# Gathering slot rows for a mixture of experts: GpSimd no longer waits for each batch of gathers, SyncE waits for the batches and counts them

## What is computed

```python
g, idx = jax.lax.top_k(logits, 2)
gates = jax.nn.softmax(g, axis=-1)
# gates_full[n, e]: the gate of token n for expert e, 0 where e was not chosen
def body(acc, p):
    W1 = wf1 + mg1 * ws1 + hf1
    h = jnp.square(jnp.maximum(flat_x @ W1 + bb1, 0.0))
    W2 = wf2 + mg2 * ws2 + hf2
    return acc + ge[:, None] * (h @ W2 + bb2), None
```

## Time and profile before

| | |
|---|---|
| device time, median of 3 (lowest, highest) | 1060.32 us (1057.99, 1063.25) |
| device time of the profiled execution | 1058.72 us |
| its span in the profile | 1057.0 us |
| TensorE busy | 789.1 us, 75% of the span |
| VectorE busy | 734.7 us, 70% |
| ScalarE busy | 650.3 us, 62% |
| GpSimd busy | 648.9 us, 61% |
| mean granted TensorE clock | 0.894 of full speed |
| first gather of slot rows starts | 791.66 us |
| last scatter starts | 1036.77 us |

### The profile page before, as it was taken

One profiled execution on the slowest core, in us unless ns is written; L12 is line 12 of the kernel. 1 busy time (PEld: TensorE's weight loads), 2 busy tenths in 40 slices (PEclk: granted clock), 3 DMA queues, 4 the chain that ended last, 5 costly groups with the idle time before them and its releaser, 6 DMA issues. The chain is left out here.

```text
span 1057.0 us, 14281 instructions
## 1 busy us (share of the span) xinstructions
PE 789.1 (75%) x4918; PEld 640.0 (61%) x4919; DVE 734.7 (70%) x836; ACT 650.3 (62%) x1149; POOL 648.9 (61%) x359
## 2 busy tenths in 40 slices
PE   0559772887878878788887888557266988999991
PEld 0225331787767777787777777457154665777771
DVE  4898376999999999999999999763182111222224
ACT  0134886999999999899998999034141221222221
POOL 7436464799988999799998999222036454111110
PEclk9969665899999999899999999887558998999996
DMA  4012101121214112122121211699996721000005
GB/s 84 0 60 119 65 25 40 41 80 61 81 60 140 61 62 79 67 74 71 70 78 63 79 63 60 215 261 238 209 206 126 160 59 42 19 19 19 19 19 187
DMA packets 31902, 91.92 MB, mean 87 GB/s; under 512 B 7560, under 2 KB 15264, under 8 KB 30824
## 3 DMA queue, kind: packets, MB, share of 16 engines
q1 hardware_dynamic: 20792, 57.53, 16.4%
q0 software_dynamic: 8352, 27.07, 11.9%
q10 hardware_dynamic: 2704, 6.61, 1.9%
HBM read 77.67 MB, written 13.53 MB: 86 GB/s over the span
## 5 line engine op out<-in xcount | busy, mean ns | idle before, releaser
L1361 PE MATMUL ps<-ident,arena 128*128 128x128 f32 (+1 forms) x3390 | 435.3, 283 | 171.2 <-DVE arena L816 54.3
L1361 PEld LDWEIGHTS ps<-ident,arena 128*128 128x128 f32 (+1 forms) x3390 | 383.4, 144 | 230.7 <-issue 73.8
L557 POOL TENSOR_TENSOR arena<-arena 128x1024 f32<-128x1024 f32 x192 | 426.5, 2250 | 44.4 <-DVE arena L816 42.1
L816 DVE TENSOR_TENSOR_SCAN arena<-arena,ps 128x1024 f32<-128x1024 f32 x192 | 427.8, 2269 | 5.3 <-PE ps L1361 3.4
L1202 ACT ACTIVATE arena<-arena,neg_a 128x510 f32<-128x510 f32 x384 | 241.2, 710 | 0.0
L1031 DVE TENSOR_SCALAR ln_in<-ps 128x768 f32<-128x768 f32 x39 | 37.3, 958 | 138.4 <-PE ps L1605 117.0
L1188 ACT ACTIVATE arena<-arena 128x384 f32<-128x384 f32 x224 | 116.6, 602 | 8.5 <-PE ps L1361 8.3
L1605 PE MATMUL ps<-arena 96*128 (+1 forms) x312 | 114.9, 512 | 8.0 <-issue 4.4
L1188 ACT ACTIVATE arena<-ln_in,arena 128x384 f32<-128x384 f32 x224 | 116.8, 608 | 6.2 <-PE ps L1361 6.1
L616 POOL DMA_INDIRECT y_rows<-arena x39 | 37.8, 968 | 133.9 <-DVE arena L1036 126.7
L1605 PEld LDWEIGHTS ps<-arena 96*128 96x128 f32 (+1 forms) x312 | 58.7, 198 | 45.0 <-issue 15.8
(11 more groups left out here) (203 smaller groups left out, 772.5 us busy)
## 6 DMA issues: line engine op xcount, KB each, us to landing
arena<-b_rows SPq DMA_DIRECT2D x64, 512.0 KB, 3.6
arena<-ws SPq DMA_DIRECT2D x16, 576.0 KB, 9.5
arena<-wf POOLq DMA_DIRECT2D x16, 576.0 KB
arena<-hf POOLq DMA_DIRECT2D x16, 576.0 KB
gates_dram<-arena SPq DMA_DIRECT2D x4, 1536.0 KB, 5.1
arena<-gates_dram ACTq DMA_DIRECT2D x3, 1536.0 KB, 13.2
arena<-y_rows SPq DMA_DIRECT2D x4, 768.0 KB, 7.2
arena<-gates_dram SPq DMA_DIRECT2D x1, 1536.0 KB, 8.9
```

The source lines that it names most:

```text
L557: g_.tensor_tensor(state[i % STATES], state[i % STATES], c_bc[u % C_BUFS], ALU.mult).then_inc(s_mul, 1)
L816: v.tensor_tensor_scan(o, a, x, 0.0, ALU.mult, ALU.add).then_inc(s_scan, 1)
L1361: return mm(o, src, ident[at:at + parts, at:at + parts], start=start, stop=True, is_transpose=True, skip_group_check=True)
```

## The change

GpSimd issues the gathers of a batch and goes on at once. Each batch has its own semaphore, and SyncE, behind its loads of slow weights, waits for the six semaphores in turn and raises `s_slot_in` by the number of slots. Nothing is changed in what is computed, in the order of the DMAs on GpSimd, or on the other three engines.

```diff
-        s_gather = sem("slot_gather_done")
+        s_gather = [sem(f"slot_gather_done_{i}") for i in range(len(BATCHES) - 1)]
...
+            for b, (first, end) in enumerate(zip(BATCHES, BATCHES[1:])):
+                sp.wait_ge(s_gather[b], 16 * (end - first))
+                sp.sem_inc(s_slot_in, end - first)
+
             sp.wait_ge(s_o2, SLOTS + 1)
             sp.wait_ge(s_scatter, 16 * SLOTS)
...
-            def gather(first, end):
-
-                for s in range(first, end):
+            def gather(b):
+
+                for s in range(BATCHES[b], BATCHES[b + 1]):
                     g_.indirect_dma_start(out=slot_rows[:, s, :], out_offset=None, in_=x_rows,
-                                          in_offset=bass.IndirectOffsetOnAxis(ap=src_row[:, s:s + 1].bitcast(U32), axis=0)).then_inc(s_gather, 16)
+                                          in_offset=bass.IndirectOffsetOnAxis(ap=src_row[:, s:s + 1].bitcast(U32), axis=0)).then_inc(s_gather[b], 16)
...
-            for b, (first, end) in enumerate(zip(BATCHES, BATCHES[1:])):
-                gather(first, end)
-                pool.wait_ge(s_gather, 16 * end)
-                pool.sem_inc(s_slot_in, end - first)
+            for b in range(len(BATCHES) - 1):
+                gather(b)
                 if b == 1:
                     for e in (LATE + 2, LATE + 3):
                         add_fast(e)
```

## The result

The changed kernel takes 1066.02 us at the median of 13 runs (1060.61 to 1069.73), the kernel before 1060.32 us beside it (13 runs, 1057.99 to 1064.7). The ratio is 1.0041, with a 95% interval of 1.0024 to 1.0058: **slower by 0.4%**, less than the 0.5% named in the prediction, and real. The profiled execution took 1065.62 us with a span of 1063.9 us, 6.9 us over the one of before. The first product of slot 38 starts at 1034.28 (chain of waits), and in the trace of before at 1027.50: 6.8 us, so all of it lies ahead of the expert loop's end.

What follows compares the result with a forecast made beforehand. TensorE bounds the expert stage, losing 19.0 us by slot 14 while GpSimd issues gathers and scatters. Start -2.0 and longer burst +6 sum to +4.0, 1064 us on the median; range 1050 to 1076.

Steps and rivals of the forecast that it cites:

- one long burst in place of three: Batch 5, batch 6 and scatters issued by GpSimd without pause, 29 us: 16.9 us lost where 10.2 were.
- start (slot 1 or 2): Batch 2 no longer waits for batch 1 and starts 2.9 us sooner; TensorE's slot 1 gains 2.0 us.
- batches 3 and 4: GpSimd's bursts for these gathers stay as long as they were, so their loss on TensorE does not change: 0.
- batches 5, 6 and scatters, without the clock: Merged GpSimd burst: 22.5 us beyond 6.5 at 0.75 us per us, +6.7, less 0.7 for fewer ready scatters: +6.
- lower clock in the stalls: Two TensorE products at the lower clock cost 4.3 us before; left unchanged, bounds -4.3 and +4.
- The lower clock I leave at its 4.3 us: TensorE's loss from two products at the lower clock taken as unchanged, bounds 0 (-4.3) and as long as the burst (+4).
- What is late next is TensorE's own work, which ends at 804.9: At slot 1, once batch 2 lands sooner, TensorE's own work limits the gain to 2.0 of 2.9 us.
- The queue's dates: On GpSimd: Hebbian weights at about 816, batch 5's first gather at about 832, gathers and scatters to about 861.
- stops the loop: Slower rival: past 6.5 us nothing gets through until the burst ends, +13 us, 1073 us; chance 0.20.
- past its first 6.5 us: A GpSimd burst passes about 6.5 us without harm, then signals come late until it is over.
- The price per burst: Faster rival: each GpSimd burst costs something when it ends, so merging saves, 1052 us; chance 0.18.
- Moved about: Rival: loss is per indirect DMA and stays near 19 us, at most 2.0 gained at the start, 1058 to 1060; chance 0.22.

Runs made afterwards that it cites:

- e11: The changed kernel, no edit, timed where the kernel before takes 1059.24 us: 1068.35 us, ratio 1.0103.
- e4: Kernel of e3 with 16 more indirect gathers in a row into unused rows behind scatter 3: 1045.6 us (one run).
- e5: The changed kernel, no edit, run where the kernel before takes 1046.32 us: 1044.36 us (one run).
- e8: The edit of e3 again, where the kernel before takes 1046.32 us: 1045.84 us, ratio 0.9987.
- e2: The changed kernel with the three small slot tables, expert numbers among them, in partition 64 instead of 0: 1039.72 us (one run).
- e3: The changed kernel with gathers spread, after the first ten one behind each scatter, SyncE waiting for weights too: 1046.22 us, ratio 1.0003 to the kernel before.
- e12: The edit of e3 a third time, where the kernel before takes 1059.32 us: 1044.63 us, ratio 0.9881.
- e1: The changed kernel with expert 0 for every slot and no register load of expert numbers by TensorE: 1035.41 us (one run).
- e9: The changed kernel with all 39 expert numbers loaded ahead of the slots, up to eight words a load, slot loop written out: 1079.24 us, ratio 1.0195.

## Why the prediction was right

The time was within 2 us of the forecast, and the term that the forecast rested on came out: one long burst in place of three costs more than they did. That the sum came so close is luck. Up to slot 14 (896.79 in the earlier trace rows, 903.46 after) its other terms were wrong, by errors that cancel: at slot 2, ahead of the long burst, the kernel was already 4.1 us late where 2.0 us of gain stood in the sum.

| term | forecast | measured |
|---|---|---|
| start (slot 1 or 2) | -2.0 | +4.1 at slot 2 |
| batches 3 and 4 (slots 2 to 8 before, with small pieces; 2 to 5 after) | 0 | about -2.8 (4.5 before, 1.7 after) |
| batches 5, 6 and scatters, without the clock | +6 | +6.7 (10.2 before, 16.9 after) |
| lower clock in the stalls | 0 | -1.3 (4.3 before, 3.0 after) |
| sum | +4.0 | +6.7 in the trace; +4.3 by the ratio |

The 16.9 of after: slots 5 to 8 take 36.19 us where 16.3 would do, 19.9 lost, of which 3.0 are products at the lower clock (5.48 and 3.22 in place of 2.85 each). In e11 the same row of 19 DMAs, 831.3 to 854.9, costs 21.3 us (slot 5 at 833.34, slot 7 at 865.56).

**The start failed.** Batch 2 does land sooner. ScalarE's copy of slot 2, at 806.07 in the earlier trace rows, is at 802.28 here:

```profile
802.28 0.36 ACT L1318 ACTIVATE arena<-arena 128x192 f32<-128x192 f32 x1 [3.83 <-SPq L480]
```

But slot 1 starts at 807.71 and not at 805, and its product takes 5.39 us against 2.85. Two steps failed. One is "The lower clock I leave at its 4.3 us": it had no term for slots 0 and 1, although the first of them ran at the lower clock in the trace of before. The windows of TensorE (length, busy, granted clock, DMA share, GB/s) have it:

```profile
800.00:810.00 10.00, 7.75 (x19) 0.67 0.88 162
810.00:820.00 10.00, 10.00 (x39) 0.77 1.04 215
```

The granted clock is 0.67 and 0.77 of full speed there, where the trace of before had 0.90 and 1.00; 0.50 is the lower of the two levels, 1.2 GHz. TensorE had stood idle ahead of slot 0's transposes for 6.5 us in the trace of before and for 8.0 us here. Slot 1 starts 0.75 us later than before: slot 0 began 0.5 us later, its product took 5.48 instead of 4.73, and 1.58 us of "issue" follow (a register load of 1.49 us, at 805.47) where there were 2.06 of waiting. Slot 1's product adds 2.5 us, the rest of the slot 0.8. I can't put this down to the change: slot 1 is at the lower clock in e4, e5, e8 and e11 too, and at the full one in e2, e3 and e12, and no edit sorts them: e3, e8 and e12 are one kernel. Nor does the idle time ahead of slot 0 sort them: 6.4 to 6.6 us in e5, e8 and e11 as in e3 and e12, 7.4 in e2. What sets the moment at which the clock rises stays open.

The other is "What is late next is TensorE's own work, which ends at 804.9". Slot 1 came out near 805 in e11 (805.16) and e12 (805.12), but their first gathers also began 1.3 us sooner (790.33 and 790.30). From first gather to slot 1 it is 15.30 us before and 14.83 and 14.82 in these two: 0.5 us gained, not 2.0. What is next behind slot 0's transposes is the load of the expert number. It took 0.33 us before, inside the wait of 2.06 us; it takes 0.83 us in e11 and 1.48 us in e12, up to 804.4. The fast weights now start 6 us sooner, and the DMA share from 800 to 810 us is 0.88 where it was 0.36. Without loads (e1) slot 1 follows slot 0 after 6.84 us, where e12 takes 8.27. The sum had no term for it.

**The queue's dates were right.** Hebbian weights 814.43 and 817.20 (forecast 816), batch 5 at 831.58 (832).

**The burst was shorter and worse.** It ended at 855.2, not 861: with TensorE held up, 4 scatters were ready and not 8. The text had allowed 0.7 us for that. Beyond its first 6.5 us it lost 16.9 us in 17.1, nearly all, where I took 0.75 per us of 22.5. The product came out the same. The second rival, "stops the loop", was thus right in its rate for this burst: what saved the sum from its +13 is that a loop that stops also ends the burst. The pauses between the bursts had been worth more than they cost. As for "past its first 6.5 us": it holds for this burst (slot 5 starts on time at 834.60), but it is no rule. After the change GpSimd issues from 790.66 to the end of batch 4 at 829.1 with one pause of 0.82 us, 38 us over slots 0 to 4, and the only "remote" waits there are two of 4.6 and 4.4 us that end at 830.9, on ScalarE's square and VectorE's `keep`. Weights are in flight all that time (DMA share 0.9 to 1.0 from 800 us on, against 0.3 to 0.4 in the long burst). Whether that is why the row does less harm is open.

**The rivals.** The price per burst falls with the 18.4 us of one slot. "Moved about" falls too: fewer DMAs in rows, more lost. Slot 15 was due at about 906 and is at 908.87, 5.44 us a slot from there as said.

**What stays open.** Below "TensorE's signals are late" no run reaches. The Trainium skill's guess on crowded SBUF ports ("DMA: Bandwidth & Descriptors", Latency and other measured facts), which the prediction took up by way of the register load, isn't borne out for the load (e9, and loads of 0.30 us in the stall), and nothing here shows a port. Whether only indirect DMAs do it, whether it needs GpSimd as issuer, and what makes a set quiet or stalling, wasn't tried or can't be seen. That e12 is faster because the rows are gone is the plain reading, but e12 also issues the gathers later and lets SyncE wait for weights, and these were not tried apart. Where nothing stalls the same edit, these two included, was worth nothing (ratios 1.0003 in e3 and 0.9987 in e8).

## What to carry to other kernels

Taking a wait out of a queue is worth only what its later work was late, and it packs what follows closer; look at what the pauses were good for. Where an engine starts late although its input was long there ("remote", "another core or an unknown queue" on one core), set the times beside the rows of GpSimd's DMAs, and spread these over the loop, one or two a step. And run the unchanged kernel beside each experiment: for the first eight kernels here the effect in question wasn't on the chip at all. The Trainium skill advises to issue a DMA early and wait late ("DMA: Bandwidth & Descriptors", Rules for kernel authors); here, on stalling chips, the kernel that issues a gather ten slots ahead and no sooner was 1.2% faster, and the one that issues all as early as it can was 0.4% slower.

## What the hardware showed that I had not expected

- One kernel takes 1059 to 1060 us in three sets and 1046 us in two, with single runs within 0.5% of these. By the traces of the changed kernel the difference is in TensorE's signals during GpSimd's DMAs. A chip's number doesn't tell which: 14 came up in a quiet and in a stalling set, though it need not be the same chip.
- Within a row of small GpSimd DMAs an increment by TensorE can come 12 to 20 us late, while those of ScalarE (846.31 for an end at 846.30, after the change) and VectorE (839.41 for 839.39, e11) come at once; four of them then rise within 0.21 us (after the change), some 1.5 to 5 us after the row's end (1.5 in e9, 3.4 after the change, 4.8 in e11).
- A register load from SBUF on TensorE takes 0.30 us by its record, and 0.64 us with its range check. Eight words at once cost 0.59 us each, all told. While weights keep the DMA engines busy one load takes up to 2.3 us (after the change) or 2.9 us (e5).
